# Second attention of a two-layer attention and mixture kernel: moving the shift rows, the division and the row copies between engines, and taking the transpose of the maxima a step later

## The reference, cut to what matters

```
q = (rms(xn)*g @ w_q) * rf     # 16 heads of 8 columns
k = (rms(xn)*g @ w_k) * rf     # 4 key heads, each used by 4 query heads
v =  rms(xn)*g @ w_v
attn = softmax(q k^T / sqrt(128))          # 512 x 512 per head, no mask
s = attn v ;  out = s + s @ w_o
x = x + out + (one of 8 experts of xn)
```

## Time and profile before

| | us |
|---|---|
| median of 3 runs | 1653.48 |
| lowest and highest | 1649.02, 1654.18 |
| span of the profiled execution | 1651.9 |
| second attention: first and last exponential begin at | 595.6, 1437.0 |
| second expert part: first loads of rows begin at | 1461.1 |

### The profile page before, as it was taken

The page is one execution under the profiler, slowest core; times in us unless marked ns, Lnnn a source line. Parts: engine busy times, 40 slices in busy tenths (PEclk is TensorE's granted clock), DMA queues, the critical chain, the costliest instruction groups (busy, mean ns, idle before and its releaser), DMA issues. The chain is left out here.

```text
span 1651.9 us, 30013 instructions
## 1 busy us (share of the span) xinstructions
PE 1455.9 (88%) x9488; PEld 716.9 (43%) x9488; DVE 1180.7 (71%) x3123; ACT 946.4 (57%) x1805; POOL 833.9 (50%) x941
## 2 busy tenths in 40 slices
PE   3999999969993279999999999999999999849996
PEld 1444444469993123333333333333333332239996
DVE  3688777833334568899889998899989998514443
ACT  2565556524441147777777778777777777612221
POOL 4688888743003463556555655556565620114443
PEclk9999999979997569999999999999999999969998
DMA  1111211289995111122112221122212210347771
GB/s 38 46 56 54 64 56 49 80 242 298 304 296 145 57 56 46 56 77 73 55 55 65 78 61 54 57 75 73 59 55 62 70 51 13 108 155 239 236 241 58
DMA packets 144965, 165.76 MB, mean 100 GB/s; under 512 B 29073, under 2 KB 115217, under 8 KB 142649
## 3 DMA queue, kind: packets, MB, share of 16 engines
q1 hardware_dynamic: 92377, 74.76, 15.2%
q10 hardware_dynamic: 38608, 58.62, 11.6%
q0 software_dynamic: 13824, 30.47, 6.0%
HBM read 111.93 MB, written 51.30 MB: 99 GB/s over the span
## 5 line engine op out<-in xcount | busy, mean ns | idle before, releaser
L1592 DVE TENSOR_REDUCE c_mx<-c_ps_mx 128x1 f32<-128x512 f32 x1024 | 649.8, 683 | 89.6 <-PE c_ps_mx L1828 82.1
L1496 ACT ACTIVATE c_pt<-c_ps_e 128x512 f32<-128x512 f32 x1024 | 567.1, 601 | 189.9 <-PE c_ps_e L1798 176.3
L1798 PE MATMUL c_ps_e<-c_qst,c_kex 74*128 74x512 bf16 (+1 forms) x1024 | 347.7, 388 | 3.5 <-ACT c_pt L1496 1.9
L1811 PE MATMUL c_ps_v<-c_pt,c_vp 128*32 128x512 f32 x2048 | 274.5, 608 | 1.1 <-ACT c_pt L1496 0.7
L1333 POOL DMA_INDIRECT c_gy<-ys,mt x128 | 124.2, 970 | 276.5 <-PE c_ps_v L1811 129.9
L1828 PE MATMUL c_ps_mx<-c_kex,c_qst 64*128 64x512 bf16 x1024 | 204.6, 396 | 57.9 <-DVE c_mx L1592 40.9
L1828 PEld LDWEIGHTS c_ps_mx<-c_kex,c_qst 64*128 64x128 bf16 x1024 | 49.3, 93 | 367.8 <-DVE c_mx L1592 345.3
L998 PE MATMUL f_ps_h<-f_xT,f_w 128*128 128x256 f32 x800 | 197.0, 386 | 0.2 <-DVE f_xT L1064 0.2
L558 ACT ACTIVATE a_pt<-a_ps_s,temp 128x1024 f32<-128x1024 f32 (+3 forms) x128 | 113.1, 884 | 91.3 <-PE a_ps_s L652 86.3
L499 POOL DMA_INDIRECT xs<-a_xn,a_meta x128 | 135.6, 1059 | 38.1 <-issue 35.3
L998 PEld LDWEIGHTS f_ps_h<-f_xT,f_w 128*128 128x128 f32 x800 | 145.4, 194 | 15.9 <-issue 0.6
(11 more groups left out here) (225 smaller groups left out, 1895.0 us busy)
## 6 DMA issues: line engine op xcount, KB each, us to landing
f_w<-in_we ACTq DMA_DIRECT2D x80, 321.0 KB, 4.4
f_w<-in_we ACTq DMA_DIRECT2D x37, 576.0 KB, 4.5
c_qst<-qparts SPq DMA_DIRECT2D x75, 192.0 KB
f_x<-rows SPq DMA_DIRECT2D x40, 257.0 KB, 3.9
f_x<-xs SPq DMA_DIRECT2D x80, 128.0 KB, 4.4
ys<-f_y ACTq DMA_DIRECT2D x80, 128.0 KB, 4.3
qparts<-c_qp SPq DMA_DIRECT2D x16, 384.0 KB, 2.5
x<-in_x SPq DMA_DIRECT2D x16, 256.0 KB, 3.0
```

The costliest lines, as they stand in the source:

```text
L1496: nc.scalar.activation(pt[:, s % 4, hl, :], ps_e[:, e_bank(64 * b + n)], ACT.Exp, scale=QSCALE).then_inc(exp_done, 1)
L1592: nc.vector.tensor_reduce(mx[:, g % 2, col:col + 1], ps_mx[:, m_bank(64 * b + 2 * m + par)], AX, ALU.max).then_inc(mx_done, 1)
L1798: nc.tensor.matmul(ps_e[:, e_bank(64 * b + n)], kex[rows, p, k_head(hl), kt * P:(kt + 1) * P], qst[rows, p, q_head(g, hl), :], start=True, ...
L1811: last = nc.tensor.matmul(ps_v[32 * hl:32 * (hl + 1), :], vp[:, p, kt, hl, :], pt[:, s % 4, hl, :], start=kt == 0, stop=kt == NT - 1)
```

## The change

- `shifts` goes from VectorE to ScalarE, as one copy of 32 rows with factor -1. The split in a high and a low part is made before the transpose, by two new operations of GpSimd on 16 columns (`split`), and `max_columns` becomes one bfloat16 product of 32 columns. It stands in the middle of step 1 and at the end of steps 5, 9 and 13.
- `normalise` is taken apart: ScalarE copies the token rows out of PSUM (`token_copy`, four a batch), VectorE takes one reciprocal of all 64 (`inverses`, step 2), GpSimd multiplies once (`normalise`, between `v_rows` and `norms`).
- The copies into the output rows (`keep_x1`, `keep_xn`, slots and token numbers) go away: `combine`, `normal_rows` and an `iota` write straight into `c_row`, which gets four buffers instead of two.
- Pieces of `c_ps_j` move: `x_rows` to the end of step 7, the two `project` to the middle of steps 8 and 9 (behind j0), `s_rows` and `s_project` to 3 and 4, `q_columns` to 12, the first `token_rows` of a batch to 6. On ScalarE `xT_copy` stands behind the first exponential of step 8, the first `prj_copy` behind the last one of step 8.

```diff
@@ POOL
+                def split(i, o, g):
+                    b, h, p = batch(i, o)
+                    pool.wait_ge(mx_done, 16 * (4 * b + g + 1) + 2)
...
+                    nc.gpsimd.tensor_copy(mxp[:, g % 2, 0], mx[:, g % 2]).then_inc(split_steps, 1)
+                    pool.wait_ge(split_steps, 4 * b + g + 1)
+                    nc.gpsimd.tensor_tensor(mxp[:, g % 2, 1], mx[:, g % 2], mxp[:, g % 2, 0], ALU.subtract).then_inc(split_ready, 1)
+                def normalise(i, o):
+                    b, h, p = batch(i, o)
+                    pool.wait_ge(rcp_ready, b + 1)
+                    pool.wait_ge(sT_ps, b)
...
                 def body(i, o):
                     prev, nxt, nxt2, nxt3 = flags(i, o)
+                    if not prev or not nxt2:
+                        split(i, o, 1)
                     if nxt2:
                         combine(ln, i, o + 2)
                     if nxt:
                         v_rows(i, o + 1)
-                    keep_xn(i, o)
+                    if prev:
+                        normalise(i, o - 1)
                     if nxt2:
                         norms(ln, i, o + 2)
+                    split(i, o, 2)
...
                     if nxt3:
-                        gather(i, o + 3, (5, 6, 7), 15)
+                        gather(i, o + 3, (5, 6), 15)
+                        split(i, o + 1, 1)
+                        gather(i, o + 3, (7,))
@@ ACT
+                def token_copy(i, o, g):
+                    b, h, p = batch(i, o)
+                    act.wait_ge(ot_ps, 4 * b + g + 1)
+                    if g == 0:
+                        act.wait_ge(all_ready, b)
+                    nc.scalar.activation(raw[:, :, g], ps_j[:].rearrange("p (t h c) -> p t h c", t=NT, h=HL)[:, :, :, 0:DH1 + 1],
+                                         ACT.Copy).then_inc(ot_sb, 1)
+                def shifts(i, o, g):
+                    b, h, p = batch(i, o)
+                    act.wait_ge(mt_ps, 4 * b + g + 1)
...
                         exps(i, o, s, 0)
-                        if s == 7 and nxt2:
+                        if s == 2 and prev:
+                            token_copy(i, o - 1, 3)
+                        if s in (7, 11, 15):
+                            token_copy(i, o, s // 4 - 1)
+                        if s in (6, 10):
+                            shifts(i, o, s // 4 + 1)
...
+                        if s == 8 and nxt2:
                             xT_copy(i, o + 2)
...
                         if s > 0 and s % 4 == 0:
                             ov_copy(i, o, s // 4 - 1)
...
-                        if s == 7 and nxt2:
+                        if s == 8 and nxt2:
                             prj_copy(i, o + 2, 0)
@@ PE
                         maximum(i, o, s, 0)
-                        if s == 7 and nxt2:
-                            free = x_rows(free, i, o + 2)
+                        if s == 1:
+                            free = max_columns(free, i, o, 1)
+                        if s in (8, 9) and nxt2:
+                            free = project(free, i, o + 2, s - 8)
...
                         if s == 7 and nxt2:
-                            free = project(free, i, o + 2, 0)
-                        if s == 9 and nxt2:
-                            free = project(free, i, o + 2, 1)
+                            free = x_rows(free, i, o + 2)
```

More of the change, by code:

```diff
@@ L1095 @@
 RING = 3
+ROWS = 4
 AHEAD = 8
@@ L1452, in body @@
                         gather(i, o + 3, (2,), 12)
+                    if nxt:
+                        split(i, o + 1, 0)
                     if nxt2:
@@ L1473, in _ @@
                 v_rows(0, 0)
+                tokens(0, 0)
                 combine(ln, 0, 1)
+                tokens(0, 1)
                 norms(ln, 0, 1)
                 normal_rows(0, 1)
+                split(0, 0, 0)
                 pool.wait_ge(const_in, 48)
@@ L1555, in body @@
                             exps(i, o, s, hl)
+                            if s == 1 and hl == 1:
+                                shifts(i, o, 1)
+                            if s == 9 and hl == 1 and nxt2:
+                                prj_copy(i, o + 2, 1)
                         if s == 0 and prev:
@@ L1572, in _ @@
                     xT_copy(0, o)
+                    if o == 1:
+                        shifts(0, 0, 0)
                     prj_copy(0, o, 0)
@@ L1696, in body @@
                         more = s + AHEAD < 16 or nxt
-                        if s == 4 and prev:
+                        if s == 5 and prev:
                             output(i, o - 1)
```

183 lines of the change are left out of this document (79 added, 104 removed).

## The result

The changed kernel takes **1696.64 us** (median of 4 runs, 1692.01 to 1697.77) against 1653.83 (4 runs, 1649.02 to 1654.84) of the kernel before: ratio **1.0253**, 95% interval 1.0230 to 1.0277. It is slower by 43 us. Its profiled execution spans 1696.1, that of before 1651.9.

A forecast was written before the change was run, and what follows sets the result against it. TensorE was taken to set the pace, waiting some 2.3 to 2.8 a batch on VectorE's reductions. 13 batches x 2.9 + 4.75 (first batch) + 1.3 (end) = 43.8, added to the 1653.48 median: 1697, range 1670 to 1714.

The forecast's parts named there:

- Step 8, +0.97: First projection, mid step 8: TensorE waits 0.97 us a batch for xT_copy, queued behind the step's first exponential.
- Step 9, +1.4: Second projection, mid step 9: TensorE waits 1.4 us a batch for the first prj_copy, behind an exponential and ov_copy.
- The rest of steps 6 to 15: Per batch: token_rows moved in +0.44, three waits gone -0.75, cheaper maxima -0.1, nearly empty ends of steps 5, 9, 13 +0.8.
- three waits: TensorE's waits of 0.2 to 0.3 in steps 7, 9 and 13 were to go, -0.75 a batch.
- Steps 0 to 5, +0.15: VectorE's relief is eaten because statistics waits for GpSimd's delayed combine: +0.15 a batch, from -0.2 to +0.5.
- The split, 0.6: Two GpSimd split operations ahead of the last gather delay it by 0.56 to 0.74, taken as 0.6.
- GpSimd's product, 1.06 by the row of the same size: GpSimd's product with the reciprocals takes 1.06, ends at 930.3 before s_rows asks at 931.1: covered.
- The forecast's rival: GpSimd's product takes 2.3 by the skill's rule, holding TensorE 0.35 a batch, 5 in all: 1702; no chance given.
- VectorE some 65 less busy: Sign expected in the profile after: VectorE's busy time falls by some 65.
- First batch, +4.75 (2 for the hold): First batch: split of group 1 holds TensorE 6.2 at step 1, net +2, plus +2.75 for steps 6 to 15.
- The end, +1.3: At the kernel's end ScalarE, VectorE and GpSimd in a row replace two VectorE operations of 0.54: +1.3.
- only the copies in time: 1662: Rival: copies of x and projection on time, steps 6 to 15 cost +0.4 a batch; 1662 to 1680 had chance 0.10.

The follow-up runs named there:

- x1_copies: Changed kernel with xT_copy behind the last exponential of step 7 and the first prj_copy ahead of ov_copy on ScalarE; 1677.02 us, ratio to before 1.0152.
- x2_ends: Changed kernel with both projections at the ends of steps 8 and 9, their ScalarE copies moved to match, max_columns(3) mid step 10; 1667.44 us, 1.0088 to before.
- x3_split: Changed kernel with GpSimd's split of the next batch's group 1 behind the last gather instead of ahead of it; 1697.98 us, ratio to before 1.0280.
- x4_four: Changed kernel with the 64-column reciprocal taken as four of 16, three in steps 8, 12 and 15, the last in step 2; 1692.56 us, 1.0245 to before.
- x6_all: x2_ends plus the four reciprocals of x4_four and the first batch's group 1 split ahead of GpSimd's k and q parts; 1661.60 us, ratio to before 1.0056.
- the three y kernels: y1_xrows, y2_rows and y3_both, all edits of the kernel before; ratios to it 0.9972, 0.9991 and 0.9966.
- y1_xrows: Kernel before with only the transposes of x moved from the middle of step 7 to the end of step 6; 1647.51 us, ratio 0.9972.
- y2_rows: Kernel before with only the rows and token numbers written directly into the output rows (four buffers), their copies dropped; 1651.10 us, ratio 0.9991.
- y3_both: Kernel before with the edits of y1_xrows and y2_rows together; 1646.37 us, ratio 0.9966.

## Why the prediction was right, and where its steps were not

The forecast was 1697, the time is 1696.6, and a batch takes 55.68 where 55.8 was forecast. Step by step:

- **Step 8, +0.97.** Right in place, cause and size. TensorE was to start the projection at T8 + 1.6, and T8 + 1.65 it is (1020.35 to 1022.00), released by the copy of x; by the starts the wait is 1.02, by the profile's count 0.94. x1_copies and x2_ends show that the place of the copy and that of the projection make it.
- **Step 9, +1.4.** The moment is right, T9 + 2.0 forecast and T9 + 1.97 measured (1024.83 to 1026.80), released by the copy of the projection. The wait in front of it is mis-sized: 0.95 (1.02 by the starts), not 1.4. j0 of this step itself waits 0.25 for its reduction, so TensorE comes to the projection at T9 + 0.95 and not at T9 + 0.63.
- **The rest of steps 6 to 15: +0.44, -0.75, -0.1 and +0.8, +0.39 together.** Cut as the forecast cuts them, from e0 of step 6 to e0 of step 16, these steps take 34.58 against 31.94: +2.64 where +2.75 was forecast. Less the two waits of 1.02 that leaves +0.60. What failed is one of the "three waits" that were to go, the one in step 9: `max_columns` left the end of step 8 and nothing took its place, so j1 of 8 is 1.18 before and after, and j0 of 9 waits. This error and the one at the projection of step 9 nearly cancel: 0.32 of what was forecast as a wait at the projection is spent at j0 instead. The prices at the ends of steps 5, 9 and 13 were wrong in two ways that cancel too: the bfloat16 transpose takes 0.26 of TensorE's time there and not 0.05 (below), so the waits at j0 of 6, 10 and 14 are 0.06 and not 0.27. Nor is it 0.1 cheaper: the float32 transpose that it replaces took 0.11 (947.86 to 947.97 in the kernel before).
- **Steps 0 to 5, +0.15.** From e0 of step 0 to e0 of step 6 they take 21.09 against 20.88, +0.21: about the right size for a wrong reason, and this is the step of the mechanism that failed. "The relief is real, and the combine chain eats it": the trace shows no idle time of VectorE ahead of `statistics`, and in x3_split the chain ends 0.7 ahead of it instead of 0.4, and step 3 doesn't change. The forecast put the reciprocal at about 0.3, from a row of 16 columns, 247 ns. At 64 columns it takes 0.55, and that fills the same slot. x4_four gives the 0.30 back. j1 of step 3 waits 0.58 where 0.9 was forecast. The chain can bind: in the kernel before, in the batch after batch 6, the last gather landed later and `statistics` did wait 0.47 for `combine` (at 981.95), and that batch took 53.40. In batch 6 of neither kernel does it.
- **The split, 0.6.** Two operations of 0.21 and 0.22, with their hand-overs 0.66 from its start to the gather's (995.77 to 996.43). Right. The last gather begins 0.34 later in the batch than before, and the chain had the room.
- **GpSimd's product, 1.06 by the row of the same size.** It takes 1.08. It begins at 1004.57, held 0.35 by the reciprocal, and TensorE waited for it once, at the very end. The forecast's rival doubled VectorE's four small products, 4 x 0.29 = 1.16, which made 2.3. The Trainium skill (GPSIMD Engine Reference, section 4.1, Engine selection) has two-input elementwise work about twice as slow on GpSimd. At equal shape the rows come near it: one operation of VectorE with two inputs of 128x512 takes 0.69, GpSimd's product takes 1.6 times that, and its addition, 1.27, 1.8 times (lines in the last section). So the rule is not refuted here; it was applied to four small operations.
- **VectorE some 65 less busy.** 57: the reciprocal again, 16 x (0.55 - 0.3) = 4 of the 8 that are missing.
- **First batch, +4.75 (2 for the hold).** It is +2.9. The hold of 6.28 is as forecast, but only 0.3 of it is net, as x6_all shows. The size of the difference is not firm: the three y kernels have first batches of 56.6, which is 0.6 to 1.0 less than the 57.77 of before less their own gains.
- **The end, +1.3.** The first loads of the second expert part come 26.7 behind the last exponential, 24.1 before: +2.7. The timeline of the end of the last batch in the kernel after:

```profile
1482.64 0.56 DVE L1663 RECIPROCAL c_rcp<-c_raw 128x64 f32<-128x64 f32 x1 [16.29 <-ACT c_raw L1545]
...
1483.29 1.06 POOL L1387 TENSOR_TENSOR c_sall<-c_raw,c_rcp 128x512 f32<-128x512 f32 x1 [17.88 <-DVE c_rcp L1663]
...
1484.50 0.63 PE L1863 MATMUL c_ps_j<-ident,c_sall 128*128 128x128 f32 x4 [2.22 <-POOL c_sall L1387]
...
1485.90 2.05 PE L1939 MATMUL c_ps_j<-wo,c_sT 128*128 128x128 f32 x8 [0.78 <-ACT c_sT L1597]
```

From the transposes of the last outputs to those of the normalised rows 2.85 pass (1481.65 to 1484.50), in the kernel before 1.40 (1439.55 to 1440.95). That is +1.45, the forecast's term. Another 0.9 stands in the next step: `s_project` takes 2.05 at a granted clock of 0.50, which is TensorE's lower level of 1.2 GHz, and in the trace of before it took 1.13 at 1.00. The 2.22 of idle time ahead of the transposes suggests itself as the cause, but the other traces speak against it. In y1_xrows, which has the chain of the kernel before, the same eight products come behind idle times of 0.77 and 0.78 and take 2.05 as well:

```profile
1434.68 0.63 PE L1840 MATMUL c_ps_j<-ident,c_sall 128*128 128x128 f32 x4 [0.77 <-DVE c_sall L1614]
1436.09 2.05 PE L1915 MATMUL c_ps_j<-wo,c_sT 128*128 128x128 f32 x8 [0.78 <-ACT c_sT L1546]
```

So it is in y2_rows and y3_both, while in x4_four, behind 1.91 idle, they take 1.34. Of the ten traces that of before is the only one at full clock there. The 0.9 is therefore no cost that can be put down to the change, and what decides the clock at this place is not shown.

So the misses were +0.06 a batch in steps 0 to 5, -0.11 in steps 6 to 15, -1.9 in the first batch and, by the span, +0.8 at the end, and the start of the profiled execution added 3.0 that belongs to no term. The 13 batches come to +35.9 and not to 13 x 2.85 = 37.1, because some of those of before are longer than 52.83 in its trace (53.18, 53.40). By the stretches that the change touches the difference is 41.2, by the medians 42.8, and the forecast had 43.8. That the total came out within a microsecond is partly luck: the first batch and the start are each off by more than that, and within a batch wrong prices cancelled. (Two sums of the forecast are slightly off without bearing on it: 14 x 1.5 below 1697 is 1676, not 1674, and 931.5 is 0.4 behind 931.1, not 0.35.)

What stays open: the rival "only the copies in time: 1662" was tried nearly as x1_copies (1677) and as x2_ends (1667). With the projection in the middle of the step the copies are late even at their earliest place tried, and at the ends the transpose in step 10 takes its share. The relief of VectorE without the other moves (the shifts and the division alone, on the order of TensorE before) was not tried either; y2_rows takes only the row copies. And why the stretch up to the second attention varies by up to 8 between executions is not shown.

## What to carry to other kernels

Ask first which engine the waiting work stands behind. Here TensorE and VectorE pass a buffer to and fro with a round trip of 1.18, and 57 us less work on VectorE did not shorten it. Work on the pacing engine costs its excess over such a round trip when it stands inside it, and all of itself elsewhere: moving four transposes from one place to another was worth 0.36 a batch, while taking work off the other engine was worth 0.20. When an operation is asked for earlier or later, follow the copy in front of it through its engine's queue, since the wait is the difference of two places and both can be read before anything is changed.

And a long operation does not cost what a short one of its kind does: take the price of the size that will run, and look which slot it lands in. The same holds the other way round when four small operations are compared with one large one on another engine.

## What the runs showed of the hardware

- **VectorE's reciprocal grew by 6.2 ns a column.** 128x16 takes 247 ns (0.24 us in x4_four too), 128x64 takes 544 ns, where the reductions do 128x512 in 685 ns. Only these two sizes ran. Groups of VectorE, the kernel after, 700 to 1300 (count | busy, mean ns | idle before):

```profile
L1656 DVE TENSOR_REDUCE c_mx<-c_ps_mx 128x1 f32<-128x512 f32 x693 | 441.0, 685 | 115.0 <-PE c_ps_mx L1851 111.0
...
L1669 DVE TENSOR_TENSOR c_row<-c_ps_j,c_row 128x512 f32<-128x512 f32 x11 | 7.6, 692 | 0.0
...
L1663 DVE RECIPROCAL c_rcp<-c_raw 128x64 f32<-128x64 f32 x11 | 6.0, 544 | 0.0
```

- **GpSimd took 1.6 to 1.8 times VectorE's time for two inputs of 128x512**: 1078 ns for the product with a spread-out factor and 1267 ns for an addition, against 692 ns for VectorE's addition above, which reads one input from PSUM. An operation of 128x16 took GpSimd 206 to 219 ns (the split). The same stretch by shape, GpSimd:

```profile
L1350 POOL TENSOR_TENSOR c_row<-c_gsum,xb 128x512 f32<-128x512 f32 x11 | 13.9, 1267 | 0.9
...
L1387 POOL TENSOR_TENSOR c_sall<-c_raw,c_rcp 128x512 f32<-128x512 f32 x11 | 11.9, 1078 | 3.0 <-DVE c_rcp L1663 2.8
```

- **A tiny transpose between score products is not free.** Step 5 of the kernel after: from the score product at 1013.49 to the next at 1013.98 pass 0.49, where 0.23 passes from e3 to the next e0 without it. So 0.26 for 32 columns at the end of a step, while four float32 transposes of 128 add 0.44. In the middle of step 1 it adds 0.16 (j0 of 1, 2.02 against 1.86).

```profile
1013.49 0.39 PE L1821 MATMUL c_ps_e<-c_qst,c_kex 128*128 128x512 bf16 x1
1013.81 0.23 PE L1916 MATMUL c_ps_j<-ident_b,c_mxp 128*32 128x128 bf16 x1
1013.98 0.39 PE L1821 MATMUL c_ps_e<-c_qst,c_kex 74*128 74x512 bf16 x1
```

At the end of a step the round trip hides it all: j1 to j0 is 1.18 there with and without it (j1 of 5 and j1 of 8 in the kernel after).
